# Gated columns and gathered rows turned by transposing SyncE transfers, with a second `gup` bank and a second product in five matmuls

## What is computed

```python
xn = _layernorm(x, axis=-1)
x = x + _L0_attn_ref(xn, Wq, bq, Wk, bk, Wv, bv, Wo, bo) + _L0_ffn_ref(xn, ...)
# _L0_ffn_ref, x: 4096 x 256, expert width I = 176
g = jnp.einsum('th,ehi->tei', x, w_gate)
u = jnp.einsum('th,ehi->tei', x, w_up)
a = jax.nn.silu(g) * u
a = a * combine[:, :, None]            # zero but for the 4 chosen experts
y = jnp.einsum('tei,eih->th', a, w_down)
y = y + jax.nn.silu(x @ sw_gate) * (x @ sw_up) @ sw_down
```

## Time and profile before

| | us |
|---|---|
| timed runs: median of 3 | 1179.19 |
| timed runs: lowest, highest | 1176.25, 1183.7 |
| the profiled execution: span from its first to its last instruction | 1354.9 |

### The profile page before, as it was taken

The page is one execution under the profiler, slowest core; times in us unless marked ns, Lnnn a source line. Parts: engine busy times, 40 slices in busy tenths (PEclk is TensorE's granted clock), DMA queues, the critical chain, the costliest instruction groups (busy, mean ns, idle before and its releaser), DMA issues.

```text
span 1354.9 us, 26394 instructions
## 1 busy us (share of the span) xinstructions
PE 1007.9 (74%) x8634; PEld 525.7 (39%) x8634; DVE 866.0 (64%) x1784; ACT 654.5 (48%) x1219; POOL 579.2 (43%) x531
## 2 busy tenths in 40 slices
PE   2788121010399999898998989998988989899885
PEld 1555010000144444444544444454444445444433
DVE  6888831000288887777777676676767676677553
ACT  3778100000154545565566666556666665566341
POOL 6333177776200000454366666435656553464100
PEclk9888555555599999899999999999989999899888
DMA  6899450010113131443545355354535353444702
GB/s 175 270 297 283 125 180 1 1 34 1 43 56 105 54 104 48 88 85 75 89 80 112 63 111 95 66 89 78 111 57 112 56 112 64 88 71 73 134 17 31
DMA packets 99484, 126.41 MB, mean 93 GB/s; under 512 B 24873, under 2 KB 83514, under 8 KB 98834
## 3 DMA queue, kind: packets, MB, share of 16 engines
q0 software_dynamic: 41632, 60.79, 25.0%
q1 hardware_dynamic: 57730, 63.99, 16.1%
HBM read 71.63 MB, written 57.80 MB: 96 GB/s over the span
## 4 chain that ended last, share of the span: by engine, by line
PE 53%; DVE 10%; another core or an unknown queue 10%; issue 9%; ACT 2%; SPq 1%; DMA 1%; POOL 0%; ACTq 0%; DVEq 0%
PE gup L1221 12%; PE pvp L1144 10%; PE outs L1248 9%; DVE part L1314 6%; PE smp L1100 6%; PE turn L1233 4%; PE stp L1125 4%; PE outs L1151 3%; PE turn L1191 3%; PE smp L1083 1%; ACT probs L1484 1%; DVE hf L1371 1%; DVE sg L1366 1%; DMA Qs<-nm 1%
## 5 line engine op out<-in xcount | busy, mean ns | idle before, releaser
L1484 ACT ACTIVATE probs<-stp 128x1024 f32<-128x1024 f32 (+1 forms) x320 | 300.4, 939 | 424.4 <-remote 205.2
L1314 DVE TENSOR_REDUCE part<-smp 128x2 f32<-128x256 f32 (+2 forms) x372 | 345.9, 951 | 140.0 <-remote 72.5
L942 POOL DMA_INDIRECT XG<-xrow_d,slots x144 | 146.8, 1019 | 247.0 <-DMA out<-Y 201.7
L1221 PE MATMUL gup<-gu_w,XC 128*128 (+1 forms) x1152 | 212.8, 321 | 32.7 <-issue 21.8
L1100 PE MATMUL smp<-Ks,Qs 48*128 48x128 f16 (+2 forms) x744 | 112.5, 341 | 103.7 <-DVE part L1314 52.4
L1248 PE MATMUL outs<-dn_w,h 88*128 (+1 forms) x1248 | 183.6, 280 | 0.1
L949 POOL DMA_INDIRECT out<-Y,slots x72 | 117.1, 1626 | 139.1 <-ACT Y L1517 107.8
L1144 PE MATMUL pvp<-probs,Vs 128*32 128x512 f32 (+3 forms) x1536 | 168.8, 512 | 0.8 <-DVE probs L1413 0.7
L949 POOL DMA_INDIRECT acc_d<-Y,slots x72 | 114.7, 1594 | 123.7 <-ACT Y L1517 104.6
L1221 PEld LDWEIGHTS gup<-gu_w,XC 128*128 128x128 f16 x1152 | 107.2, 99 | 96.1 <-issue 43.5
L931 POOL DMA_INDIRECT slot_d<-entry,slot_i x128 | 124.3, 971 | 41.6 <-issue 41.6
(11 more groups left out here) (170 smaller groups left out, 1109.6 us busy)
## 6 DMA issues: line engine op xcount, KB each, us to landing
rb<-rsum_d SPq DMA_DIRECT2D x60, 128.0 KB
Ks<-k_d SPq DMA_DIRECT2D x96, 64.0 KB
Qs<-q_d SPq DMA_DIRECT2D x96, 64.0 KB
v_d<-V SPq DMA_DIRECT2D x8, 544.0 KB, 4.6
Vs<-v_d SPq DMA_DIRECT2D x16, 272.0 KB, 3.0
acc_d<-YA SPq DMA_DIRECT2D x1, 4224.0 KB
X<-L_attn_x POOLq DMA_DIRECT2D x8, 512.0 KB, 5.0
xrow_d<-XR SPq DMA_DIRECT2D x8, 512.0 KB, 5.0
```

Source lines behind the costliest of these rows:

```text
L942: pool.indirect_dma_start(XG[:, q].rearrange("p a c t -> p (a c t)"), None, s.xrow_d, bass.IndirectOffsetOnAxis(ap=slots[:, r, 0:1], axis= ...
L1221: last = pe.matmul(gup[:, 0:2 * I], columns[:, a, h], weights_of(s.gu_w, e, b, h, slice(0, 2 * I)), start=n == 0, stop=n == 5)
L1314: last = dve.tensor_reduce(part[:, g % 2, k0 // CH, :, j, t], banks[:, :, col:col + w], AX.X, ALU.max)
L1484: act.activation(to, of, ACT.Exp, scale=float(DK) ** -0.5 / QS ** 2).then_inc(exp_done, 1)
```

## The change

Both turnings leave PE. SP issues a transposing DMA from `XG` to `XC` for every gathered tile (`columns`, three units ahead, `LEAD`; four `XC` buffers, five `XG` buffers instead of eight) and one from the new `HX` to the new `HT` for every unit. For that ACT makes the float16 high part of `hf` in the slot after the first half (`HIGH`), token by token and before the turning; DVE subtracts the low part in the slot after that (`LOW`), in two instructions, because `HX` holds 384 columns: 128 high, then 48 high, 16 of zeros and 48 low, padded to 128, then 128 low. SP issues the transfer in the same slot. `LAG` becomes 3. The down weights are staged in 128 rows (128 of the 176, then the last 48 twice), so an expert takes five DMAs instead of three, and the second product becomes five matmuls of 128, 128, 128, 112 and 48 rows. `gup` gets a second PSUM bank in the place of `turn`, and `th` a second buffer. The bank `turn`, `turn_rows`, `turn_h` and ACT's copy to `XC` are gone, and the planner's costs are 900 and 600 for the halves.

```diff
-                pool.dma_start(dn[:, n], d.rearrange("(c p) n -> p c n", p=IP)).then_inc(gu_in[n], 16)
+                pool.dma_start(dn[:, n, 0], d[0:P]).then_inc(gu_in[n], 16)
+                for r in (0, P // 2):
+                    pool.dma_start(dn[r:r + IT, n, 1], d[P:P + IT]).then_inc(gu_in[n], 16)
...
-        GB, AHEAD = 8, 10
+        GB, AHEAD = 5, 10
+        CB, LEAD = 4, 3
+        XC = sb("XC", [P, CB, 2, HC, P], F16)
...
-            cost = [(880 if shared_of(v) is not None else 1200, 980)[h] for h, v in halves]
+            cost = [(900, 600)[h] for h, v in halves]
...
-        LAG, SPARE = 2, 4
+        LAG, SPARE = 3, 4
+        HIGH = {divmod(k + 1, SLOTS): v for v, k in first_slot.items()}
+        LOW = {divmod(k + 2, SLOTS): v for v, k in first_slot.items()}
...
-                    pool.wait_ge(xp_done, r - GB + 1)
+                    pool.wait_ge(*columns_in(ST + r - GB))
...
+            def columns(x):
+                if x >= CB:
+                    sp.wait_ge(gu_done, LAST_UNIT[x - CB] + 1)
+                to, done = XC[:, x % CB], columns_in(x)[0]
+                if ST <= x < ST + UT:
+                    r = x - ST
+                    sp.wait_ge(xg_in[r % GB], 16 * (r // GB + 1))
+                    sp.dma_start_transpose(to.rearrange("p a c t -> p (a c) t"),
+                                           XG[:, r % GB].rearrange("p a c t -> p (a c t)")).then_inc(done, 16)
...
+            def turn_gated(v):
+                sp.wait_ge(hl_done, v + 1)
+                if v >= TB:
+                    sp.wait_ge(y_done, v - TB + 1)
+                sp.dma_start_transpose(HT[:, v % TB], HX[v % XB]).then_inc(ht_in[v % TB], 16)
...
+                    if (g, n) in LOW:
+                        turn_gated(LOW[g, n])
                     if (g, n) in FIRST:
                         after_first(FIRST[g, n])
...
             def gate_up(v):
-                if v:
-                    pe.wait_ge(hf_done, v)
+                if v >= 2:
+                    pe.wait_ge(hf_done, v - 1)
...
             def down(v, projected):
-                pe.wait_ge(hl_done, v + 1)
+                pe.wait_ge(*gated_turned(v))
...
-                for c in range(2):
-                    for a, b in PASSES:
-                        last = pe.matmul(yp, h16[:, v % 2, a, c], weights_of(s.dn_w, e, b, c, slice(0, D)),
-                                         start=begin and n == 0, stop=end and n == 5)
+                for n, (c, rows, b) in enumerate(((0, P, 0), (0, P, 1), (2, P, 0), (1, IZ, 2), (1, IT, 3))):
+                    last = pe.matmul(yp, HT[0:rows, v % TB, c], weights_of(s.dn_w, rows, e, b, slice(0, D)),
+                                     start=begin and n == 0, stop=end and n == 4)
...
                     def second_half():
-                        turn_h(z)
-                        if z:
-                            down(z - 1, projected)
-                        return outs_before(z)
+                        down(z, projected)
+                        return outs_before(z + 1)
...
             def low_part(v):
                 dve.wait_ge(hh_done, v + 1)
+                x, h = HX[v % XB], hf[:, v % FB]
+                dve.tensor_tensor(x[:, 2 * P:3 * P], h[:, 0:P], x[:, 0:P], ALU.subtract)
+                dve.tensor_tensor(x[:, P + P // 2:P + IZ], h[:, P:I], x[:, P:I], ALU.subtract).then_inc(hl_done, 1)
...
             def high_part(v):
+                act.wait_ge(hf_done, v + 1)
+                if v < XB:
+                    act.wait_ge(hx_clear, XB)
+                else:
+                    act.wait_ge(*gated_turned(v - XB))
+                act.activation(HX[v % XB][:, 0:I], hf[:, v % FB], ACT.Copy).then_inc(hh_done, 1)
```

More of the change, by code:

```diff
@@ L43, in token_mixer_with_experts @@
     HC = D // P
-    IP = I // 2
+    IT = I - P
+    IZ = P // 2 + IT
     TT = T // P
@@ L57, in token_mixer_with_experts @@
     VW = 4 * (DK + 1)
-    assert D == 256 and N % CH == 0 and I % 2 == 0 and DK == 16
+    assert D == 256 and N % CH == 0 and 0 < IT <= P // 2 and DK == 16
     nc.disable_value_cache = True
@@ L345, in expert_parts @@
             return ([one(s.gu_w[:, e, a]).rearrange("p c (a i) -> p c a i", a=2) for a in range(2)],
-                    [one(s.dn_w[:, e, a]) for a in range(2)])
+                    [one(s.dn_w[:, e, a::2]) for a in range(2)])
         @block.scalar
@@ L791, in attention_and_experts @@
         pvp = ps("pvp", [P, CH])
-        gup = ps("gup", [P, CH])
-        turn = ps("turn", [P, CH])
+        gup = ps("gup", [P, 2, CH])
         outs = ps("outs", [P, 2, D])
         mxp = smp[0:4 * KT, 0, 0:P]
-        xp = turn[:, 0:2 * P].bitcast(F16)
-        hp = turn[0:IP, 2 * P:4 * P]
         yp = outs[:, 0]
@@ L800, in attention_and_experts @@
         early = smp[:, 1, 0:D]
-        last_tiles = [stp[:, 0, 0:D], stp[:, 1, 0:D], gup[:, 0:D], turn[:, 0:D]]
+        last_tiles = [stp[:, 0, 0:D], stp[:, 1, 0:D], gup[:, 0, 0:D], gup[:, 1, 0:D]]
         SLOTS = 20
@@ L836, in shared_of, with tile_of, tiles_loaded_at, columns_in @@
             return v if v < SU else v - UT if v >= SU + UT else None
+        def tile_of(v):
+            u = shared_of(v)
+            return ST + v - SU if u is None else u // SH if u < SU else UT + u // SH
+        FIRST_UNIT = [next(v for v in range(NV) if tile_of(v) == x) for x in range(ST + UT + KT)]
+        LAST_UNIT = [FIRST_UNIT[x] + (1 if ST <= x < ST + UT else SH) - 1 for x in range(ST + UT + KT)]
+        def tiles_loaded_at(v):
+            return [x for x in range(ST + UT + KT) if FIRST_UNIT[x] - LEAD == v]
+        def columns_in(x):
+            return xc_in[x % CB], 16 * (x // CB + 1)
+        def gated_turned(v):
+            return ht_in[v % TB], 16 * (v // TB + 1)
         def outs_before(v):
@@ L924, in _ @@
             pool.memset(sel[:, :], 0.0).then_inc(a_const, 1)
+            for x in HX:
+                pool.memset(x[:, P:2 * P], 0.0).then_inc(hx_clear, 1)
             pool.wait_ge(a_const, 3)
@@ L959, in add_attention @@
                                YA[:, t0:t0 + KT // 2], accum_op=ALU.add).then_inc(added[0], 16)
-            for r in range(GB):
+            for r in range(AHEAD):
                 gather(r)
@@ L1047, in _ @@
             sp.dma_start(s.out[ST * P:T, :], s.xf[ST * P:T, :]).then_inc(cleared, 16)
+            for x in range(ST):
+                if FIRST_UNIT[x] < LEAD:
+                    columns(x)
             for t in range(2):
-                shared_columns(t)
                 shared_rows(t)
@@ L1220, in gate_up @@
                     for h in range(HC):
-                        last = pe.matmul(gup[:, 0:2 * I], columns[:, a, h], weights_of(s.gu_w, e, b, h, slice(0, 2 * I)),
+                        last = pe.matmul(gup[:, v % 2, 0:2 * I], columns[:, a, h], weights_of(s.gu_w, P, e, b, h, slice(0, 2 * I)),
                                          start=n == 0, stop=n == 5)
@@ L1295, in _ @@
             values(NG - 1, NST - 1)
-            down(NV - 1, projected)
             pe.wait_ge(ot_done, QC * (NG - 1))
-            for i, over in enumerate(((exp_done, SLOTS * NG), None, (hf_done, NV), (hl_done, NV))):
+            for i, over in enumerate(((exp_done, SLOTS * NG), None, (hf_done, NV), None)):
                 if over:
@@ L1365, in silu_times_up @@
                 dve.wait_ge(th_done, v + 1)
-                dve.scalar_tensor_tensor(out=sg[:, :], in0=th[:, :], scalar=1.0, in1=gup[:, 0:I],
+                dve.scalar_tensor_tensor(out=th[:, v % 2], in0=th[:, v % 2], scalar=1.0, in1=gup[:, v % 2, 0:I],
                                          op0=ALU.add, op1=ALU.mult).then_inc(sg_done, 1)
@@ L1416, in after_second @@
             def after_second(v):
-                u = shared_of(v - 1) if v else None
+                u = shared_of(v)
                 if u is not None and u % SH == SH - 1:
```

151 lines of the change are left out of this document (49 added, 102 removed).

## The result

The changed kernel takes 1263.1 us (median of 4 runs, 1259.4 to 1268.9), the kernel before beside it 1181.5 (1176.3 to 1187.0). The ratio is 1.070 with a 95% interval of 1.065 to 1.076: 82 us slower. The prediction had said 31 us faster, with a range that ended at 1255.

A forecast was written before the change was run, and what follows sets the result against it. PE was taken to bound the long stage. Terms -112 (work), -22 (idle), +30 (DVE), +70 (SP's queue) and +3 (preparation) gave -31 us: 1179 to 1148 us, range 1070 to 1255.

The forecast's parts named there:

- PE's work, -112: Long stage: transposes of gated columns, 54 us, of gathered rows, 35, and one of six weight loads, 23, leave PE.
- its idle time, -22: PE's waits before the removed transposes and for the one gup bank, 45 us in all; 22 taken, bounds 0 and 45.
- +30 for DVE: Long stage: two subtractions instead of one add DVE work; PE's wait for its reductions grows by 30 us, ends 16 and 43.
- PE sets the pace: Long stage, 370 to 1345 us: PE, busy 885 of 975 us (91%), was taken as the bound.
- SP's queue, +70 with ends 28 and 112: Head group's turn: SP's backlog delays gated columns; PE waits 5 us a group (2 to 8) in 14 groups.
- the slack: Two slots, 5.1 us, less 1.3 for ACT and DVE, leave 3.8 for a 3 us landing: hidden, just, if SP is free.
- SP as the bound, from 1.6 us an issue: Rival: SP's group work reaches 58.3 us at 3.2 us a pair; 1254 us at 1.83 an issue; chance 0.28.
- 110 to 170: Sign to be shown: PE's busy time in the long stage falls by 110 to 170 us.
- Carried over one to one, the empty stretch left out: Profile 176 us longer than timed runs, mostly the empty 192 us stretch; long-stage differences carried over unscaled.
- Preparation, +3: Preparation: two more DMAs an expert land weights some 1.5 us later, mostly covered; +3 us, ends 0 and 27.
- A regular transfer's speed: Skill's claim on transposing DMAs: landing would be 2.4 us, not 3, and the sum 8 us lower, 1140.
- The rival from the Trainium skill's page: Transposes go one at a time: 1309 ns per 128x128, as a rate 1560 us for all transfers; chance 0.06.

The follow-up runs named there:

- e16: Changed kernel with LAG 4, SP's turn loads spread over slots, and plain transfers of the same bytes instead of transposing ones: 1131.1 us, ratio 0.957.
- e5: Changed kernel with LAG 4 instead of 3, four HT buffers, and SP's loads at a turn spread over slots: 1197.4 us, ratio 1.015.
- e12: Changed kernel, its own order kept, with plain transfers of the same bytes instead of the 352 transposing ones: 1209.4 us, ratio 1.021.
- e9: Kernel before with only the five-matmul second product, DVE's one subtraction kept, low part of the last 48 columns left out: 1169.8 us, ratio 0.991.
- e7: Kernel before with only the five-matmul second product, both transposes on PE, DVE's subtraction in two parts: 1189.7 us, ratio 1.009.
- e6: Kernel before with only the gathered rows turned by SP's transposing transfers, and SP's turn loads spread over slots: 1174.5 us, ratio 0.995.
- e17: Changed kernel with LAG 4, spread loads and plain transfers, each block cut into three transfers and each tile of rows into two: 1271.7 us, ratio 1.074.
- e11: Changed kernel with four matmuls of no use ahead of PE's wait for each routed unit's turned block: 1280.9 us.
- second profile of before: Kernel before, unchanged, run and profiled once more for an execution of ordinary length: 1186.4 us, a single run.

## Why the prediction was wrong

The runs give the 82 us in three pieces, each as a difference to the kernel before of its own session. Both halves of the change with plain transfers and slack in the order: -50 (`e16`). Transposing transfers in their place: to +19 (`e5`), so 69 more. The change's own order, `LAG` 3 and twelve loads at a turn: to +82, 63 more. Taken the other way round, order before price, the last two are 76 (`e12` against `e16`) and 56. The new planner costs and the five `XG` buffers, for which POOL stood 70 us, are in `e16` too, so they do not carry the loss. Not parted were the second `gup` bank and the clock. Against the prediction's sum:

- **PE's work, -112, and its idle time, -22, with +30 for DVE: -104 together; about half of it came.** The step that failed is the first one: "PE sets the pace", read from 91% busy. `e9` tests it without any transfer: -23 gave -10. DVE is on the path as well: its 0.155 us a unit cost 21 us where PE's 0.11 gained 10 (`e7`, `e9`). With SP's part made small, 50 us came off the end (`e16`); some of the missing 54 is still SP's there, as two waits of `e16` from 400 to 1100 us show (below; 3.1 and 0.2 us before the change). `e6` gave 4 for 35, but with 144 transposing transfers in its queue. DVE's own work was sized rightly, 281 + 202 ns a unit in the change against 417, 0.07 us more as estimated. PE's wait for `part` grew from 11 to 35 us in 700 with the change, which is the +30 of the sum over the 920 us of the earlier trace rows; but where `HT` was in time it grew to 60 (`e16`) and 88 (`e5`), when the sum allowed 59 over 920 at most.

```profile
DVE OT L1350 <- DMA rb<-rsum_d: 21.8, 10, 4.1
...
PE stp L1168 <- DMA Qs<-nm: 19.2, 10, 9.3
```

- **SP's queue, +70 with ends 28 and 112: the mechanism was right, its size was not.** Price and order together made 132. The `XC` issue was guessed at 1.2 us and measured 1.22; the `HT` issue at 1.0 and measured 1.19; the landing at 3 and measured 3.6 on the chain. The waits cluster at the turn as foretold: 95 us over 15 groups in slots 0 to 5 are 6 a group, inside "2 to 8". The backlog reaches further, though, into slot 7 behind the reciprocals' wait, 24 us more, which makes it 8 a group where 5 were taken. 15 us are one wait near the end, 8 lie elsewhere. The failing term is the slack: "just" enough for 3 us was not enough for 3.6 behind a queue, and it took the longer lag and the spread loads together to win back 63 us. And once PE no longer waited for `HT`, DVE waited for the reciprocals of the same queue (`e5`), which the sum didn't hold.
- **SP as the bound, from 1.6 us an issue.** The rival's working (a pair at 3.0 us is 14.0 + 3.5 + 12.6 x 3.0 = 55 us a group) stays under the 58.3 at which it was to be the bound, yet in `e17`, at that price and with smaller packets, most groups take 63 to 70 us. This in-order queue, which also waits for its own landings and for DVE's blocks, cost time long before its work filled the group. With this point set too high, the slower side got 0.34 and the range ended at 1255.
- **TensorE's clock was not in the sum at all.** The same first-product matmul takes 341 ns in the mean against 320 in the two 400 to 1100 stretches, 7%, and so PE's busy time over the whole execution fell only from 1004 to 942 us, 62, where "110 to 170" was to be shown. If PE had been on the path all the time, that would be 942 x 7% or some 60 us (an estimate); what part of it is real stays open (`e11`).
- **Carried over one to one, the empty stretch left out: right.** It is not in the second profile of before. **Preparation, +3: nothing.** The first product starts at 197.4 us with the change and at 197.6 without.
- **A regular transfer's speed.** The prediction cited the Trainium skill, "Advanced Engine Details and Errata", section "X-Bar Transpose (TRN2)": transposing DMAs as fast as regular ones. This case's traces disagree in what mattered: for a block 1.19 us of SP an issue against 0.47, 3.6 us to the landing on the chain against 3.0. The rival from the Trainium skill's page "VectorE: DVE Perf Modes", section "The three transpose paths", read as a rate that forbids overlap, did not come about either: 352 transfers of 3.6 us one at a time would be 1267 us, and the stage that holds them ran from 197 to 1240, 1043 us.

## What to carry to other kernels

A busy share of 91% did not make PE the bound here, with its neighbours' waits short and many. Before counting on such a share, take a little work from it in a cheap run first, and see how much of it reaches the end. When work moves to a DMA queue, count what each issue holds the issuing engine for, and give every consumer slack for a queue, not for one transfer; then spread the other loads of that queue; here only both together brought back most of the loss. And when a wait is removed, look where it went before calling it gone.

## What the runs showed of the hardware

A transposing transfer of 128 x 384 or 128 x 512 two-byte elements held SP for 1.19 or 1.22 us, against 0.47 or 0.55 for a plain one of the same bytes. Its packets are many: 222,594 on the queue instead of 108,418 with plain transfers, and the DMA engines' busy share in 400 to 1100 us went from 0.62 to 0.81 for the same bytes. That load is not needed for the loss: plain transfers cut into pieces, with the DMA engines at 0.60, were slower still, but these too had more packets and held SP for longer (3.0 us a pair). TensorE's granted clock in 400 to 1100 us was 0.98 in the second profile of before, and 0.88 to 0.93 in the runs in which PE stood longest (0.89 with the change, 0.93 in `e5`, 0.88 in `e17`); it rose by 0.03 when matmuls of no use were put ahead of the waits (`e11`).
